# Attention of a graph and transformer kernel: values in native fp32 on two column halves, a maximum in two steps, a score pass on row halves

## The reference, cut to attention

```python
q = (xq @ Wq + bq).reshape(N, 8, 64) * 64 ** -0.5
k = (xk @ Wk + bk).reshape(N, 8, 64)
v = (xv @ Wv + bv).reshape(N, 8, 64)
att = softmax(einsum('thd,shd->hts', q, k), axis=-1)   # temporal: keys after t are masked
o = einsum('hts,shd->thd', att, v).reshape(N, 512)
```

## Time and profile before

| | us |
|---|---|
| median of three runs | 3688.52 (3687.89 to 3691.71) |
| the profiled execution | 3685.27 |
| its span, first to last instruction | 3683.3 |
| busy: TensorE matmul / VectorE / ScalarE / GpSimd | 2924.3 / 2123.6 / 1642.9 / 1118.4 |

### The profile page before, as it was taken

The page is one execution under the profiler, slowest core; times in us unless marked ns, Lnnn a source line. Parts: engine busy times, 40 slices in busy tenths (PEclk is TensorE's granted clock), DMA queues, the critical chain, the costliest instruction groups (busy, mean ns, idle before and its releaser), DMA issues. The chain is left out here.

```text
span 3683.3 us, 45803 instructions
## 1 busy us (share of the span) xinstructions
PE 2924.3 (79%) x15443; PEld 2179.4 (59%) x15443; DVE 2123.6 (58%) x3892; ACT 1642.9 (45%) x3566; POOL 1118.4 (30%) x1141
## 2 busy tenths in 40 slices
PE   0404675999965996869999698878999899998798
PEld 0201223887854774534444586768788787887676
DVE  6103554477853112559999437763688647886533
ACT  0100002477731552546666426652677536775322
POOL 4776663556302443156666000000000000001210
PEclk9756776999985998889999799999999999999899
DMA  3104564723114996354443264214422043311322
GB/s 102 34 6 134 171 172 137 180 54 57 22 54 144 332 344 213 130 195 135 147 137 95 80 195 106 53 49 135 113 51 61 8 146 101 68 44 39 94 71 77
DMA packets 231418, 413.01 MB, mean 112 GB/s; under 512 B 48860, under 2 KB 146442, under 8 KB 227092
## 3 DMA queue, kind: packets, MB, share of 16 engines
q1 hardware_dynamic: 174532, 273.61, 25.2%
q0 software_dynamic: 56208, 136.40, 13.6%
q10 hardware_dynamic: 448, 0.08, 0.0%
HBM read 318.32 MB, written 95.47 MB: 112 GB/s over the span
## 5 line engine op out<-in xcount | busy, mean ns | idle before, releaser
L916 DVE TENSOR_TENSOR at_s<-at_pb,at_s 125x500 fp32r<-125x500 f32 (+1 forms) x864 | 482.7, 584 | 199.8 <-ACT at_s L829 188.7
L829 ACT ACTIVATE at_s<-at_pb 125x500 fp32r<-125x500 f32 (+1 forms) x864 | 447.8, 519 | 283.8 <-PE at_pb L746 277.6
L746 PE MATMUL at_pb<-ident,at_p 125*125 125x125 f32 x2880 | 479.5, 281 | 34.6 <-ACT at_p L844 14.2
L746 PEld LDWEIGHTS at_pb<-ident,at_p 125*125 125x125 f32 x2880 | 417.9, 190 | 133.0 <-DVE at_s L916 72.0
L763 PE MATMUL at_pb<-at_s,at_v 125*128 125x250 f32 x2880 | 483.8, 296 | 7.7 <-DVE t_t L928 3.9
L906 DVE TENSOR_REDUCE at_max<-at_pb 125x1 f32<-125x1250 f32 (+4 forms) x320 | 423.0, 1322 | 12.9 <-PE at_pb L731 8.1
L844 ACT ACTIVATE at_p<-at_pb,at_max 125x1250 f32<-125x1250 f32 (+4 forms) x320 | 382.6, 1196 | 28.6 <-DVE at_max L906 27.0
L763 PEld LDWEIGHTS at_pb<-at_s,at_v 125*128 125x128 f32 x2880 | 383.4, 191 | 14.7 <-DVE at_s L916 7.2
L1356 PE MATMUL so_ps<-g_got,g_hot 128*125 128x512 f32 x332 | 185.5, 710 | 239.5 <-DMA g_got<-support,g_edges 170.3
L708 PE MATMUL at_pb<-at_s,at_shared 128*128 128x500 f32 (+1 forms) x1152 | 230.0, 362 | 63.2 <-DVE at_shared L866 63.2
L1356 PEld LDWEIGHTS so_ps<-g_got,g_hot 128*125 128x125 f32 x332 | 68.7, 221 | 356.3 <-issue 347.5
(11 more groups left out here) (303 smaller groups left out, 5498.6 us busy)
## 6 DMA issues: line engine op xcount, KB each, us to landing
w_ring<-in_L_ffn_w SPq DMA_DIRECT2D x128, 512.0 KB
at_shared<-k_parts SPq DMA_DIRECT2D x64, 312.5 KB
ml_w<-in_mlp_w SPq DMA_DIRECT2D x64, 256.0 KB
k_parts<-at_shared SPq DMA_DIRECT2D x64, 250.0 KB
q_parts<-at_shared SPq DMA_DIRECT2D x64, 250.0 KB
h_edges<-em_both SPq DMA_DIRECT2D x11, 1024.0 KB
g_h<-h_edges SPq DMA_DIRECT2D x11, 1024.0 KB
at_shared<-q_parts SPq DMA_DIRECT2D x32, 312.5 KB
```

Source lines behind the costliest of these rows:

```text
L746: ins = pe.transpose(pturn[0:TN, g % 2, TN * (t % 4):TN * (t % 4) + TN], p[:, u % 2, TN * t:TN * t + TN], c.ident[0:TN, 0:TN])
L829: act.activation(p_hi[:, u // 2 % 2, 4 * n:4 * n + m, TN * (u % 2):TN * (u % 2) + TN], pturn[0:TN, g % 2, 0:TN * m].rearrange("p (a b) -> ...
L916: dve.tensor_tensor(p_lo[at], pturn[0:TN, g % 2, 0:TN * m].rearrange("p (a b) -> p a b", b=TN), p_hi[at].bitcast(F32), ALU.subtract).then_ ...
```

## The change

- **Values.** `v` is one fp32 tile, without a low part, `p_t` one fp32 tile of weights with SBUF of its own. `duo_sum` is 10 native fp32 matmuls with 64 weight columns and 250 moving ones; even key tiles write PSUM partitions 0 to 63, odd ones 64 to 127. ScalarE's copy and VectorE's add of the halves stay. The pieces of a duo are 2, 2, 4 and 2 matmuls over four iterations.
- **Weights.** Each block of transposes is copied once: block 0, and block 2 of even units, by ScalarE, the others by VectorE (`take_part`). TensorE waits for both counts (`wait_taken`).
- **Second score pass** (not causal). For the two pieces of 512 it uses only the 64 partitions with q's high part: the piece 0 on the half where `q_two` has it, the piece 1 on the other half, where the new tile `q_swap` has it again. The first pass and the 226 columns are as before. `load_pair` loads `q_swap`, four transfers more for each pair of heads (also in the causal attention).
- **Maximum** (not causal). `wide_max` of unit s takes the 1024 columns of the first two pieces, `tail_max` the last 226 together with that result, in the next iteration.
- The low part of v in the projection is gone; its place is an empty instruction that counts. Two integer tiles of the constants are freed after use.

```diff
-        v = sb("at_v", [TN, NT, HEADS, 2, HD], F32R)
+        v = sb("at_v", [TN, NT, HEADS, HD])
...
+        q_swap = [[sb(f"at_qs{n}", [128, HN], F32R) for n in range(2)], [None, sb("at_qs2", [128, HN], F32R)]]
...
-        p_hi, p_lo = (t[0:TN, :].rearrange("p (a t q) -> p a t q", a=2, t=NT) for t in (s_hi, s_lo))
+        p_t = sb("at_pt", [TN, 2, NT, 2 * TN])
...
-        LOADS = 12
+        LOADS = 16
...
+                    for n in range(2):
+                        eng.dma_start(q_swap[j % 2][n][(low, top)[h], :].bitcast(F32), q_d[0, j, r, HN * n:HN * n + HN])                            .then_inc(sem, 16)
...
+        by_act = lambda u, n: n == 0 or (n == 2 and u % 2 == 0)
...
+                    paired = n < 2 and not causal
...
-                    ins = pe.matmul(score[u % 2][0:TN, a:b], q_two[j % 2][h][:, TN * i:TN * i + TN], k_lo[j % 2][h][:, a:b],
-                                    start=False, stop=True)
+                    if not paired:
+                        ins = pe.matmul(score[u % 2][0:TN, a:b], q_two[j % 2][h][:, q_at], k_lo[j % 2][h][:, a:b],
+                                        start=False, stop=True)
+                    elif n == 1:
+                        for (a, b), q, r in ((there[0], q_two[j % 2][h], h), (there[1], q_swap[j % 2][i // (NT // 2)], 1 - h)):
+                            at = q_at if r == h else slice(TN * (i % (NT // 2)), TN * (i % (NT // 2)) + TN)
+                            r = slice(64 * r, 64 * r + 64)
+                            ins = pe.matmul(score[u % 2][0:TN, a:b], q[r, at], k_lo[j % 2][h][r, a:b],
+                                            start=False, stop=True)
...
-                        pe.wait_ge(lo_done, g - 1)
+                        wait_taken(pe, g - 1)
...
-                    src = (p_hi, p_lo)[half]
-                    cut = keys[u] * 7 // 10
-                    for t in (range(cut), range(cut, keys[u]))[piece]:
-                        ins = pe.matmul(pout[:, 0:2 * TN], v[:, t, 2 * j + h, :, :].rearrange("p a d -> p (a d)"),
-                                        src[:, q % 2, t, :], start=(half == 0 and t == 0),
-                                        stop=(half == 1 and t == keys[u] - 1))
...
+                    cut = lambda n: 2 * round(keys[u] // 2 * n / 4)
+                    for t in range(cut(2 * half + piece), cut(2 * half + piece + 1)):
+                        side = 64 * (t % 2)
+                        ins = pe.matmul(pout[side:side + 64, 0:2 * TN], v[:, t, 2 * j + h, :], p_t[:, q % 2, t, :],
+                                        start=(t < 2), stop=(t >= keys[u] - 2))
...
-                    high_part(s - 2, 0)
-                    high_part(s - 2, 1)
+                    take_part(s - 2, 0)
...
+                def wide_max(u):
+                    a = pieces[u % 2][0][0]
+                    dve.wait_ge(wide_scored, u + 1)
+                    dve.tensor_reduce(neg_wide[:, u:u + 1], score[u % 2][0:TN, a:a + 1024], AX, ALU.max, negate=True)\
+                        .then_inc(wide_ready, 1)
...
+                def tail_max(u):
+                    a = pieces[u % 2][2][0]
+                    dve.wait_ge(scored, u + 1)
+                    dve.wait_ge(wide_ready, u + 1)
+                    dve.tensor_scalar(unused[:, 0:TAIL], score[u % 2][0:TN, a:a + TAIL], -1.0, neg_wide[:, u:u + 1],
+                                      ALU.mult, ALU.min, accum_out=neg_max[:, u:u + 1]).then_inc(max_ready, 1)
...
+                        (whole_max if causal else tail_max)(s - 1)
                     u = s - 2
...
+                    take_part(u, 1)
+                    if not causal and s < NU:
+                        wide_max(s)
+                    take_part(u, 2)
```

More of the change, by code:

```diff
@@ L528, in attention @@
         q_two = [[t[:, :] for t in front], second[0:2]]
+        q_swap = [[t[:, :] for t in q_swap[0]], [shared[:, 6 * N:6 * N + HN], q_swap[1][1][:, :]]]
         k_hi = [[k_hi_both[:, h, :] for h in range(2)], second[2:4]]
@@ L574, in attention, with wait_taken @@
         upto = lambda u: sum(turns[:u])
+        taken = [(u, n) for u in range(NU) for n in range(turns[u])]
+        by_act = lambda u, n: n == 0 or (n == 2 and u % 2 == 0)
+        act_by = lambda g: sum(1 for u, n in taken[:g] if by_act(u, n))
+        dve_by = lambda g: g - act_by(g)
+        def wait_taken(eng, g):
+            if act_by(g):
+                eng.wait_ge(act_took, act_by(g))
+            if dve_by(g):
+                eng.wait_ge(dve_took, dve_by(g))
         norms = [(j, k) for j in range(PAIRS_) for k in range(3)]
@@ L728, in score_part @@
                         pe.wait_ge(exp_done, u)
-                    pe.matmul(score[u % 2][0:TN, a:b], q_two[j % 2][h][:, TN * i:TN * i + TN], k_hi[j % 2][h][:, a:b],
+                    paired = n < 2 and not causal
+                    pe.matmul(score[u % 2][0:TN, a:b], q_two[j % 2][h][:, q_at], k_hi[j % 2][h][:, a:b],
                               start=True, stop=False)
-                    ins = pe.matmul(score[u % 2][0:TN, a:b], q_two[j % 2][h][:, TN * i:TN * i + TN], k_lo[j % 2][h][:, a:b],
-                                    start=False, stop=True)
+                    if not paired:
[7 more added lines that the diff above has]
+                                            start=False, stop=True)
                     if n == len(there) - 1:
                         ins.then_inc(scored, 1)
+                    elif n == 1 and not causal:
+                        ins.then_inc(wide_scored, 1)
                 def turn_part(u, n):
@@ L895, in _, with whole_max @@
                     dve.wait_ge(saved, 16)
+                def whole_max(u):
+                    w = TN * keys[u]
+                    dve.wait_ge(scored, u + 1)
+                    m = TN * (2 - u % 2)
+                    late = score[u % 2][0:TN, w - m:w]
+                    dve.tensor_tensor(late, late, c.causal[:, 0:m], ALU.add).then_inc(masked, 1)
+                    dve.wait_ge(masked, u + 1)
+                    dve.tensor_reduce(neg_max[:, u:u + 1], score[u % 2][0:TN, 0:w], AX, ALU.max, negate=True)\
+                        .then_inc(max_ready, 1)
@@ new lines, in take_part @@
+                def take_part(u, n):
+                    if not 0 <= u < NU or n >= turns[u] or by_act(u, n):
+                        return
+                    g = upto(u) + n
+                    dve.wait_ge(turned, g + 1)
+                    if u % 2 == 0 and u >= 4:
+                        dve.wait_ge(pv_done, u // 2 - 1)
+                    m = min(4, keys[u] - 4 * n)
+                    dve.tensor_copy(p_t[:, u // 2 % 2, 4 * n:4 * n + m, TN * (u % 2):TN * (u % 2) + TN],
+                                    pturn[0:TN, g % 2, 0:TN * m].rearrange("p (a b) -> p a b", b=TN)).then_inc(dve_took, 1)
@@ L896, in _ @@
                 for s in range(NU + 4):
                     if 1 <= s <= NU:
-                        u = s - 1
-                        w = TN * keys[u]
-                        dve.wait_ge(scored, u + 1)
-                        if causal:
-                            m = TN * (2 - u % 2)
-                            late = score[u % 2][0:TN, w - m:w]
-                            dve.tensor_tensor(late, late, c.causal[:, 0:m], ALU.add).then_inc(masked, 1)
-                            dve.wait_ge(masked, u + 1)
@@ L906, in _ @@
-                        dve.tensor_reduce(neg_max[:, u:u + 1], score[u % 2][0:TN, 0:w], AX, ALU.max, negate=True)\
-                            .then_inc(max_ready, 1)
-                    u = s - 2
-                    for n in range(turns[u] if 0 <= u < NU else 0):
-                        g = upto(u) + n
-                        dve.wait_ge(hi_done, g + 1)
-                        if u % 2 == 0 and n == 0 and u >= 4:
-                            dve.wait_ge(pv_done, u // 2 - 1)
-                        m = min(4, keys[u] - 4 * n)
-                        at = (slice(None), u // 2 % 2, slice(4 * n, 4 * n + m), slice(TN * (u % 2), TN * (u % 2) + TN))
-                        dve.tensor_tensor(p_lo[at], pturn[0:TN, g % 2, 0:TN * m].rearrange("p (a b) -> p a b", b=TN),
-                                          p_hi[at].bitcast(F32), ALU.subtract).then_inc(lo_done, 1)
+                        (whole_max if causal else tail_max)(s - 1)
@@ L2238, in program @@
         col = lambda n: c.pcol[:, PCOL[n]]
-        make_constants(nc, c)
+        with nc.sbuf_tensor("iota_i", [128, 256], I32) as c.iota_i, nc.sbuf_tensor("node_i", [128, NT], I32) as c.node_i:
+            make_constants(nc, c)
         table0, table1 = dram("table0", [128 * NS, ROW]), dram("table1", [128 * NS1, ROW])
```

35 lines of the change are left out of this document (18 added, 17 removed).

## The result

The changed kernel takes 3743.8 us (median of 4 runs, 3741.7 to 3748.3) against 3689.5 of before (4 runs, one more than in the table of before, 3687.9 to 3691.7): 1.0149 of it, interval 1.0135 to 1.0162. It is 54 us slower, where 68 us faster was forecast. The profiled execution took 3744.6 us, span 3742.9.

A forecast was written before the change was run, and what follows sets the result against it. Unmasked loops were taken as bound by a VectorE/ScalarE ring (3.78 us), TensorE just under. From 3685.3: 70 gained there (3.89 to 3.60, 240 units), 5 causal, 8 lost to loads, 3 added for the median: 3620 us, range 3510 to 3800.

The forecast's parts named there:

- What bounds the kernel before: Unmasked attention loops: a VectorE and ScalarE ring at 3.78 us, TensorE's 3.43 us just under it; units take 3.89.
- the ring: Unmasked attention, per unit: exponential, last score piece, maximum over all 1250 columns, exponential again, 3.78 us.
- Maximum in two steps: Unmasked loops: only a 226-column maximum stays late, taken 0.5 us; its ring becomes 2.6, a second ring allows about 3.0.
- Weights copied once: Transposed blocks: one copy each, VectorE's at 0.67 to 0.69 us; per unit VectorE 2.8, ScalarE 2.3, neither the bound.
- Second score pass: Unmasked loops: two half-row 512-column matmuls share one slot, scores 0.93 us per unit in place of 1.16.
- Values: Native fp32 value matmuls on column halves: partial overlap, 14 slots a duo, 1.49 us per unit, 0.32 more than before.
- rival (c): Value matmuls: column halves overlap completely; TensorE 3.10, 3.2 us per unit, 166 us gained, 3525 us; chance 0.22.
- Changes of layout: TensorE, whole array to halves and back: six changes per unit, 0 to 0.18 us each, taken as 0.
- rival (a): Layout changes cost d each, a unit takes 3.60 + 6d; at d = 0.10 about 3780 us; chance 0.23.
- The added 0.08 of waiting: Value groups wait on the previous duo's sum: 0.08 us added to TensorE's 3.52, giving 3.60 per unit.
- Causal loop: Causal attention, 80 units: 5 us gained, between 15 gained and 15 lost.
- Loads: Extra q_swap loads delay the first score at each of four loops: 0 to 4.9 us, taken 2, 8 lost in all.

The follow-up runs named there:

- e4: The kernel before with only the maximum in two steps (unmasked loops): 3607.9 us, 0.9928 of the kernel before.
- e7: e5 with the maximum in one step again: 3652.9 us, 0.9938 of the kernel before.
- e5: Changed kernel with the second score pass whole, no q_swap loads, values in two groups a duo (unmasked loops): 3610.4 us, 0.9821 of the kernel before.
- e6: e5 with all values of a duo in one group (unmasked loops): 3649.6 us, 0.9923 of the kernel before.
- e1: Changed kernel with the second score pass over all 128 rows, extra loads kept unused: 3652.8 us, 1.0053 of the kernel before.
- e3: Changed kernel with all value matmuls on one column half, order and layout changes kept: 3961.5 us, 1.0905 of the kernel before.
- e10: e5 with the extra q_swap loads back, unused: 3625.8 us, 0.9855 of the kernel before.
- e9: e5 with the tail's second score pass on only 64 rows (unmasked loops): 3696.6 us, 1.0054 of the kernel before.

## Why the prediction was wrong, point by point

**What bounds the kernel before: half right.** The maximum closed the ring in every second unit only. In the spatial loop 39 of the 80 exponentials start within 0.1 us of the end of the maximum, like the first in the earlier trace rows (2749.98, after 0.18 of waiting for it). In 40 others the maximum is 0.3 early, and the exponential follows ScalarE's second copy: so in the very unit that the prediction read, where the maximum ends at 2753.46 and the exponential starts at 2753.76, behind L829. The two kinds take 3.90 or 4.07 and 3.79. The 3.78 that was put down to the maximum is thus a second ring, through ScalarE's two copies, and e4 shows it alone. The forecast wasn't hurt by this, since the change also takes one of the copies out of that ring.

**Maximum in two steps: right.** Forecast 0.5 for the late operation, measured 0.45 and 0.08 for the read of its result. e4 takes the whole maximum out and gains 26 us, e7 puts it back into e5 and loses 42. The later of the two rings was to fall to about 3.0, and e6 shows it at 2.88.

**Weights copied once: right.** VectorE's copy takes 0.68 (0.67 to 0.69 was forecast), and neither VectorE nor ScalarE is the bound after.

**Second score pass: the mechanism right, the sum wrong.** The pair starts within 4 ns and takes one slot. But 0.235 saved stands against 0.37 for its two changes, and e1 shows the loss.

**Values: two errors, in opposite directions.** The middle taken for the overlap (14 slots a duo) was too dear: it is 10, rival (c)'s part. A group of one pair was forecast at 0.64 and of two at 1.07; with their changes they last 0.57 and 1.00 to the next layout, so the groups alone came out near the forecast by accident, and before and behind each stand 0.09 and 0.10 more.

**Changes of layout: this is the step that failed.** 0 to 0.18 was kept, and 0 was taken, by the earlier trace rows. Those rows go from 78 weight columns to 64 in transposes, and no idle follows. As the text itself allowed, it may be no change of layout. The profile gives these transposes the same 125*64 as the value matmuls, which do pay, even on one half alone (e3); what tells the two apart is in no row. The row nearest in shape was taken for the row nearest in kind. The true value was at the far end of the range, 0.177. Put into rival (a)'s formula with full overlap it gives 3.06 + 6 x 0.177 = 4.12, against 4.14 measured. Rival (a) and rival (c) were both true at once, and the cases of the prediction held each only alone: the forecast of (a) started from 3.60 and not from 3.10. By (a)'s own formula with d = 0.177 it would have been 4.66.

**The added 0.08 of waiting: wrong, and small.** Between its own matmuls TensorE waits for nothing but the changes.

**Causal loop:** 5 us gained was forecast, within 15 either way; it was 9.8.

**Loads:** the place right, the size low: 8 us forecast, 14 measured (e10, and the gaps). The bound of 4.9 a loop held.

**The sum.** 3618 + 240 x (4.14 - 3.60) = 3748, less 5 in the causal loop and 6 more for the loads, 3749; measured in that execution 3744.6. That it comes so close is in part luck: the 3.89 is from twenty units of one loop, and the unmasked loops grew by 45 us and not by 60, while 10 us between the loops are in no term of the sum.

**What stays open.** In the runs on the other chips, the loops and starts account for the difference to before within 7 to 10 us only (e5: loops 77 us shorter than in the trace of before, the time 67 us). Before was traced on one chip alone, so this can't be placed; but 10 us are missing between the traces of before and after of the first set too. What within a change takes the 0.18 (weight load, emptying of the array) was not taken apart, and no run has native fp32 values on the whole array.

## What to carry to other kernels

Halves of the array overlap fully, but each passage between whole and half costs about three quarters of a 512-column fp32r matmul: collect half-array work into few long groups, and set the saving against two changes for each group before writing it. Stop collecting where the other engines' ring makes TensorE wait in the units left without a group (e6). Look at what releases the exponential in several units in a row and not in one: here two rings took turns. When no row shows a resource, and both ends of its range decide the sign, take the likelier combination of ends and not a convenient zero.

## What the hardware showed that was not expected

- Six changes of layout a unit at 0.177 us each on average; 0.185 in e9, where nothing else was changed. Within a layout weights load under the matmul before; across a change the load starts only with its own matmul, after 0.12 to 0.38 us of idle.
- The price is the same when only one column half is used (e3).
- Native fp32 on two column halves: the records go in pairs, 6 to 7 ns apart, a pair every 0.21 us for 250 columns. Per unit that is 1.05 us against the 1.17 of the two fp32r passes before. With its changes even the best version has more TensorE work than the kernel before (3.06 + 0.235 + 0.34 = 3.64 against 3.43 us a unit); so it wins by its rings. With two ScalarE copies ahead of the exponential the ring takes 3.78 (e4), with one 2.88 (e6), and one copy is enough because native fp32 values need no low part. No run has one copy with the values of before.
